# Turning the normed output by DMA, scores in four full banks, and a new order on VectorE, in a retention + MoE block

## The reference, cut to what matters

```python
h = rmsnorm(xn); q, k, v = (h @ ternary(qkv_w).T) split in heads and chunks
def step(S, (qi, ki, vi)):
    scores = einsum('bhtd,bhsd,hts->bhts', qi, ki, mask)      # mask decays and is causal
    o = scale * (einsum('bhts,bhsd->bhtd', scores, vi) + einsum('bhtd,ht,bhde->bhte', qi, lam_t, S))
    kv = einsum('bhtd,ht,bhte->bhde', ki, lam_rev, vi)
    return lam_T * S + kv, o
out = rmsnorm(out, norm_w, 1e-6)
out = rmsnorm(out, proj_norm_w, eps) @ ternary(proj_w).T
```

## Time and profile before

| | |
|---|---|
| median of 3 runs | 1403.2 us (1401.72 to 1403.88) |
| the profiled execution, its own time | 1401.92 us |
| its span | 1400.2 us |
| PE, DVE, ACT, POOL busy over the span | 91%, 50%, 37%, 38% |
| attention steps | from about 76 to 547 us of the span |

### The profile page before, as it was taken

How to read it: one execution, slowest core, us unless ns; L and a number is a source line. 1 busy time by engine, 2 the same in 40 slices (tenths; PEclk the granted TensorE clock), 3 DMA queues, 4 the chain that set the end, 5 groups by cost and what they waited for, 6 DMA issues and landing times. The chain is left out here.

```text
span 1400.2 us, 29499 instructions
## 1 busy us (share of the span) xinstructions
PE 1281.1 (91%) x10418; PEld 879.9 (63%) x10418; DVE 695.2 (50%) x1606; ACT 514.0 (37%) x1034; POOL 527.0 (38%) x467
## 2 busy tenths in 40 slices
PE   1499999999999994999999969999999969999997
PEld 1477777667776673777777734444444447777775
DVE  4477877878878766883333322222222213333323
ACT  3444444444444434432323224544445411111111
POOL 0333344333444332024541035555554542444333
PEclk9699999999999997999999989999999989999999
DMA  5213443334433334524552358888888861443333
GB/s 173 95 60 129 154 145 109 109 131 142 161 109 109 131 125 162 180 93 105 107 138 102 33 136 183 188 194 190 186 191 186 192 190 65 179 164 135 135 136 121
DMA packets 174072, 195.06 MB, mean 139 GB/s; under 512 B 100976, under 2 KB 107248, under 8 KB 174000
## 3 DMA queue, kind: packets, MB, share of 16 engines
q1 hardware_dynamic: 158464, 156.17, 38.0%
q0 software_dynamic: 13328, 37.04, 10.0%
q10 hardware_dynamic: 2208, 0.82, 0.2%
HBM read 117.55 MB, written 56.77 MB: 124 GB/s over the span
## 5 line engine op out<-in xcount | busy, mean ns | idle before, releaser
L1269 PE MATMUL gu<-xT,WG 128*128 128x256 f16 x3072 | 350.3, 275 | 23.5 <-DMA x1s<-x_dram 11.8
L1269 PEld LDWEIGHTS gu<-xT,WG 128*128 128x128 f16 x3072 | 302.7, 99 | 74.8 <-DVE WD L1556 12.4
L1280 PE MATMUL rgu<-WG,raw 128*128 x876 | 215.1, 382 | 14.4 <-issue 10.9
L1695 DVE SCALAR_TENSOR_TENSOR actv<-gu,up_inv,sg 128x512 f32<-128x512 f32 x64 | 48.0, 751 | 252.8 <-ACT sg L1532 252.6
L1532 ACT ACTIVATE sg<-gu,gate_inv 128x512 f32<-128x512 f32 x64 | 43.9, 686 | 319.2 <-PE gu L1269 319.2
L1287 PE MATMUL yp<-WD,ah 128*128 128x512 f16 x512 | 152.3, 379 | 1.0 <-DVE al L1700 1.0
L1280 PEld LDWEIGHTS rgu<-WG,raw 128*128 128x128 f16 x876 | 86.1, 98 | 105.5 <-issue 23.2
L1850 POOL TENSOR_TENSOR xsp<-xg,xsp 128x512 f16<-128x512 f32 x75 | 86.7, 1157 | 105.2 <-ACT xsp L1918 105.2
L655 PE MATMUL ring<-hh,qkvT 128*128 128x256 f16 x512 | 116.4, 276 | 6.0 <-DVE hl L972 6.0
L1250 POOL DMA_INDIRECT xg<-xn_dram,idx x77 | 73.8, 958 | 123.9 <-POOL xsp L1850 66.4
L655 PE MATMUL ring<-hl,qkvT 128*128 128x256 f16 x512 | 116.4, 275 | 0.0
(11 more groups left out here) (237 smaller groups left out, 2163.2 us busy)
## 6 DMA issues: line engine op xcount, KB each, us to landing
y_dram<-raw SPq DMA_DIRECT2D x72, 256.0 KB
xl<-in_L_attn_x SPq DMA_DIRECT2D x16, 512.0 KB, 4.5
xn_dram<-xn SPq DMA_DIRECT2D x16, 512.0 KB, 6.4
wraw<-in_L_ffn_w_gate_up SPq DMA_DIRECT2D x16, 512.0 KB, 6.9
xT_dram<-x SPq DMA_DIRECT2D x16, 512.0 KB, 2.8
xr<-in_L_attn_x SPq DMA_DIRECT2D x16, 512.0 KB, 5.9
x_dram<-x SPq DMA_DIRECT2D x32, 256.0 KB, 2.1
xT<-xT_dram SPq DMA_DIRECT2D x16, 512.0 KB, 6.9
```

What stands on the lines that cost most here:

```text
L1269: ins = pe.matmul(gu[:, h, f * tokens:(f + 1) * tokens], w[:, kk, b, a0:a0 + P], x[:, kk, a], start=(kk == 0 and (a, b) == PASSES[0]), sto ...
L1280: ins = pe.matmul(gu[bank][:], x(kk, a), w[:, 0, kk, b, :], start=(i == 0), stop=(i == len(done) - 1))
L1695: v.scalar_tensor_tensor(out=actv[:, g % 2], in0=gu[g % 2][:, 1].rearrange("p (f t) -> p f t", f=FT), scalar=up_inv[:, 1:2], in1=sg[:], op ...
```

## The change

- `o_turn` and the ring's fills onT0 and onT1 go. ScalarE's `y_high` and VectorE's `y_low` now work on on3 in SBUF, before it is turned, and write the halves ys (128 x 2 x 512, f16); SP turns both halves at once with one DMA transpose per u (`turn_y`) into yT, for which `proj` waits. `store_xT` goes ahead of it in SP's list.
- Scores: all 16 heads of one u in the four full banks, two handovers per u and step instead of four; VectorE's product is 128 x 1024 instead of 128 x 512.
- `masked_kv` leaves VectorE; ScalarE's `take_kv` copies the four diagonal blocks (32 partitions x 4 x 32) in four activations; the rest of kvm is zeroed once by POOL.
- New orders on VectorE and ScalarE; STEP is 18 long, and the second `proj` now waits for `v0`.
- g1 and g2 are made by `tensor_scalar` instead of `tensor_tensor`.

```diff
-    STEP = ["xnT0", "xnT1", "kTr0", "ot0", "kv0", "q0", "q1", "kTr1", "ot1", "rt", "onT0", "k0", "kv1", "k1", "proj0",
-            "onT1", "v0", "v1", None, None, "proj1"]
+    STEP = ["xnT0", "xnT1", "kTr0", "ot0", "kv0", "q0", "q1", "kTr1", "ot1", "rt", "k0", "kv1", "k1", "proj0",
+            "v0", "v1", None, "proj1"]
@@ SP
+            def turn_y(u, q, par):
+                n = 2 * q + par
+                wait_apart(sp, S["yl_ready"], 2 * n + u + 1, S["sp_passed"])
+                sp.dma_start_transpose(yT[:, u], ys[:, u].rearrange("p a c -> p (a c)")).then_inc(yT_in[u], 16)
...
                     load_weights(*after(q, par))
+                    store_xT(*after(q, par))
                 for u in range(B):
-                    if u == 1 and front:
-                        store_xT(*after(q, par))
+                    turn_y(u, q, par)
+                for u in range(B):
@@ TensorE
-                o_turn(0, q, par, st)
...
-                    scores(0, *nxt, (0, 1))
-                o_turn(1, q, par, st)
-                if front:
+                    scores(0, *nxt)
                     project("v0", *nxt, st)
-                    scores(0, *nxt, (2, 3))
                     project("v1", *nxt, st)
                 proj(1, q, par, st)
@@ ScalarE
+            def take_kv(u, q, par, st):
+                n = 2 * q + par
+                bank = filled(act, f"kv{u}", st)
+                act.wait_ge(state_ready[u], n)
+                for j in range(HPT):
+                    own = slice(HD * j, HD * j + HD)
+                    ins = act.activation(kvm[own, u, :, own], bank[own].rearrange("p (g e) -> p g e", g=KT)[:, :, own],
+                                         ACT.Copy)
+                ins.then_inc(S["kvm_ready"], 1)
...
+            def y_high(u, q, par):
+                n = 2 * q + par
+                act.wait_ge(S["on3_ready"], 2 * n + u + 1)
+                act.wait_ge(yT_in[u], 16 * n)
+                act.activation(ys[:, u, 0], on3[:, u], ACT.Copy).then_inc(S["yh_ready"], 1)
...
                 o_root(0, q, par)
+                take_kv(0, q, par, st)
                 if front:
                     take("q0", *nxt, st)
                     take("q1", *nxt, st)
                 on_squares(0, q, par)
+                y_high(0, q, par)
                 take_oT(1, q, par, st)
                 o_square(1, q, par)
-                y_high(0, q, par, st)
+                o_root(1, q, par)
+                if norm:
+                    norm_roots(q + 1, par)
                 if front:
                     take("k0", *nxt, st)
-                o_root(1, q, par)
+                on_squares(1, q, par)
+                y_high(1, q, par)
                 if front:
                     take("k1", *nxt, st)
-                on_squares(1, q, par)
-                if norm:
-                    norm_roots(q + 1, par)
-                y_high(1, q, par, st)
+                take_kv(1, q, par, st)
@@ VectorE, the step as it stands after
+                scaled_k(0, q, par, st)
+                if front:
+                    h_low(*nxt)
+                decayed_scores(1, q, par)
+                o_mean(0, q, par)
+                normed(0, q, par)
+                weight_maxima(q, par, (1, 2, 3))
+                scaled_k(1, q, par, st)
+                second_norm(0, q, par)
+                y_low(0, q, par)
+                if has_norm:
+                    row_stats(0, q + 1, par)
+                    row_stats(1, q + 1, par)
+                if front:
+                    take_logits(*nxt, st)
+                if has_norm:
+                    norm_stats(q + 1, par)
+                o_mean(1, q, par)
+                normed(1, q, par)
+                if has_norm:
+                    norm(q + 1, par)
+                    norm_factors(q + 1, par)
+                second_norm(1, q, par)
+                y_low(1, q, par)
+                weight_maxima(q, par, (0,))
+                residual(0, q, par, st)
+                if front:
+                    decayed_scores(0, *nxt)
+                else:
+                    weight_scales()
+                residual(1, q, par, st)
```

More of the change, by code:

```diff
@@ L497, in attention @@
         xT_out = [sem(c, f"xT_out{i}") for i in range(2)]
+        yT_in = [sem(c, f"yT_in{i}") for i in range(B)]
         wraw_in = [sem(c, f"wraw_in{i}") for i in range(2)]
@@ L657, in project, with scores @@
                 ins.then_inc(done, 1)
-            def scores(u, q, par, sets):
+            def scores(u, q, par):
                 n = 2 * q + par
-                if u == 0 and sets[0] == 0:
+                if u == 0:
                     pe.wait_ge(S["q_ready"], 2 * n + 2)
                     pe.wait_ge(S["k_ready"], 2 * n + 2)
[L664 to L669, removed]
+                for pair in range(2):
+                    pe.wait_ge(sc_free[pair], 2 * n + u)
+                    for g in range(KT):
+                        for j in (2 * pair, 2 * pair + 1):
                             rows = slice(HD * j, HD * j + HD)
-                            ins = pe.matmul(sc[:, j, gg * P:(gg + 1) * P], kT[rows, par, g, u * P:(u + 1) * P],
+                            ins = pe.matmul(sc[:, j, g * P:(g + 1) * P], kT[rows, par, g, u * P:(u + 1) * P],
                                             qT[rows, par, g, u * P:(u + 1) * P], start=True, stop=True)
@@ L690, in outputs @@
                               start=(g == 0), stop=False, skip_group_check=True)
[L691 to L701, removed]
+                for pair in range(2):
+                    pe.wait_ge(sc_free[pair], 2 * n + u + 1)
+                for g in range(KT):
+                    for j in range(HPT):
+                        h = HPT * g + j
+                        ins = pe.matmul(bank[HD * j:HD * j + HD, g * P:(g + 1) * P],
+                                        vS[:, par, u, HD * h:HD * h + HD],
+                                        probs[:, u, j // 2, j % 2, g, :], start=False,
+                                        stop=(g == KT - 1 and j == HPT - 1), skip_group_check=True)
                 ins.then_inc(done, 1)
@@ L720, in outer @@
                 ins.then_inc(done, 1)
[L722 to L728, removed]
             def proj(u, q, par, st):
                 n = 2 * q + par
-                pe.wait_ge(S["yl_ready"], 2 * n + u + 1)
+                pe.wait_ge(yT_in[u], 16 * (n + 1))
                 bank, done = fill(pe, f"proj{u}", st)
                 for g in range(KT):
-                    for y in (yh, yl):
-                        ins = pe.matmul(bank[:], y[:, u, g, :], projT[:, g, :],
-                                        start=(g == 0 and y is yh), stop=(g == KT - 1 and y is yl))
+                    for a in range(2):
+                        ins = pe.matmul(bank[:], yT[:, u, a * KT + g, :], projT[:, g, :],
+                                        start=(g == 0 and a == 0), stop=(g == KT - 1 and a == 1))
                 ins.then_inc(done, 1)
@@ L747, in prologue @@
                     project(name, 0, 0, None)
-                scores(0, 0, 0, (0, 1, 2, 3))
+                scores(0, 0, 0)
                 for name in ("v0", "v1"):
@@ L1018, in weight_scales, with decayed_scores @@
                                        op0=ALU.mult, op1=ALU.mult)
-            def decayed_scores(u, q, par, sets):
+            def decayed_scores(u, q, par):
                 n = 2 * q + par
                 v.wait_ge(S["kscale_ready"], n + 1)
-                for s in sets:
-                    pair = s % 2
-                    v.wait_ge(sc_full[pair], 4 * n + 2 * u + s // 2 + 1)
-                    v.scalar_tensor_tensor(out=probs[:, u, s].rearrange("p (j g) t -> p j (g t)", j=2),
-                                           in0=sc[:, 2 * pair:2 * pair + 2, 0:2 * P],
+                for pair in range(2):
+                    v.wait_ge(sc_full[pair], 2 * n + u + 1)
+                    v.scalar_tensor_tensor(out=probs[:, u, pair].rearrange("p j g t -> p j (g t)"),
+                                           in0=sc[:, 2 * pair:2 * pair + 2],
                                            scalar=r[:, par, u:u + 1],
-                                           in1=mask[:, 4 * s:4 * s + 4].rearrange("p (j g) t -> p j (g t)", j=2),
+                                           in1=mask[:, 8 * pair:8 * pair + 8].rearrange("p (j g) t -> p j (g t)", j=2),
                                            op0=ALU.mult, op1=ALU.mult).then_inc(sc_free[pair], 1)
@@ L1148, in step @@
                 residual(1, q, par, st)
-                if has_norm:
-                    norm_factors(q + 1, par)
             run_steps(v, prologue, step)
@@ L1185, in prologue @@
             def prologue():
+                pool.memset(kvm[:], 0.0)
                 x_low(0, 0)
```

62 lines of the change are left out of this document (15 added, 47 removed).

## The result

The changed kernel takes **1425.53 us** (median, 1419.69 to 1427.19), the kernel before 1402.46 (1400.97 to 1403.88) beside it: a ratio of 1.0157 [1.0125, 1.0189]. So it is 23 us slower. The forecast was 1409 within 1383 to 1430, with slower as the likeliest of the three signs. The profiled execution took 1427.19 us at a span of 1425.4.

A forecast was written before the change was run, and what follows sets the result against it. TensorE's list was taken to set the period by a small margin. Its 3.0 us gain a step returns as one wait, -3 us in all, and clock falls add +10: 1409 us against the profiled 1401.9, range 1383 to 1430.

The forecast's parts named there:

- TensorE, removed: TensorE's list loses o_turn (0.88 us a step) and waits for v1 and scores (2.1): 26.5 us a step, 3.0 less.
- First half and shared wait: First u: normed ends at 10.9 us, over 1 earlier; y_low waits for POOL, starting at 14.4 instead of 14.0.
- Rival 3: POOL goes ahead of y_low, +2 us a step, +30 to +50; or transposes land late, +0.9 a step; chance 0.13.
- The transposes: DMA transposes of the normed output land 3.1 us after issue, before proj wants them, covered by 1.2 and 1.5 us.
- Second half: Second u: POOL holds norm, k1 is copied at 24.3 us, TensorE idles 3.0 before the scores; -0.2 a step.
- Rival 2: VectorE's norm in the second half is not held by POOL: 28.0 us a step, -20 us, 1383; chance 0.15.
- The clock: TensorE's idle time lowers its granted clock, 1.6 us a fall; six falls taken, +10 us, between 0 and +25.
- The likeliest case: TensorE's idle time before the scores with some falls of the clock: 1401 to 1424 us; chance 0.5.
- Rival 1: TensorE's idle time stays but the clock holds: -3 us with an error of 6, 1393 to 1405; chance 0.2.

The follow-up runs named there:

- e6: e3 with the output's turn back on TensorE and the second proj again waiting for the v copy: 1394.29 us, a step of 28.98.
- e3: The changed kernel with ScalarE taking kv1 and k1 early and norm roots last, and VectorE's norm work put behind what the turn needs: 1366.6 us.
- e4: The changed kernel with every DMA transpose issued twice, first into a spare tile: 1421.95 us.
- e9: The changed kernel with the score matmuls of one u issued over all four row groups in turn: 1404.78 us.
- e2: The changed kernel with twelve needless 512-column matmuls filling TensorE's idle time before the scores: 1404.09 us.
- e1: The changed kernel with ScalarE's copy of k1 taken ahead of the squares and y_high(1): 1382.19 us.
- e7: The changed kernel with ScalarE copying kv1 and k1 ahead of the squares and y_high(1), VectorE's order left alone: 1395.52 us.

## Why the prediction was right, and where its sizes were off

**TensorE, removed.** Right: 0.88 of transposes and the wait for v1 are gone, and put back they cost 1.95 a step (e6). I had laid out 26.5 us for TensorE with nothing else to wait for; it is 27.03 (e3), mainly since the scores of one u take 1.65 and not 1.34. That term was twice the 0.67 of sixteen in the earlier trace rows; the pace of sixteen matmuls did not hold for thirty-two.

**First half and shared wait.** Right. The product of 1024 columns takes 1276 ns where I took 1.28. `y_low`(0) and POOL:

```profile
368.82 1.27 POOL L1162 TENSOR_TENSOR state<-state,kvm 128x512 f32<-128x512 f32 x1
...
369.66 0.98 DVE L1074 TENSOR_TENSOR ys<-on,ys 128x512 f16<-128x512 f32 x1
...
370.06 2.80 POOL L1150 TENSOR_TENSOR qlam<-qT,lamq 128x1024 f32<-128x1024 f32 x1
```

`y_low` sits until POOL's L1162 is through (recorded end 370.09) and then runs: 0.98 for the 0.69 that `y_low`(1) takes at 348.00, where POOL is idle. It ends 15.35 behind the second `proj` at 355.29 (laid out: 15.1). POOL's next is 2.80 long instead of the 2.35 of the earlier trace rows: now POOL waits for VectorE. Rival 3, in which POOL goes ahead, is refuted. The Trainium skill (SBUF — State Buffer, "Who interferes with whom") states that a VectorE instruction with two SBUF inputs contends with a GpSimd one that reads SBUF. The 0.98 for 0.69 agrees, for an instruction of 512 columns.

**The transposes.** Right: 3.1 from issue to landing at the median, 4.1 at most (the other half of rival 3, a late landing, is out too), no wait of `proj` in the steady steps, and two of them in a row cost nothing either (e4). Four small copies take 1.09, 0.27 each, where I took 0.26.

```profile
L580 SPq DMA_TRANSPOSE yT<-ys x32: 1232/1242/1422, 91.0 to 558.5; - x32
...
DMA to landing us min/median/max: 3.0/3.1/4.1
```

**Second half.** Right in every link. `norm` was held and ended at 21.8 as laid out (344.39 + 1.88 - 324.41 = 21.9); z2(1) came at 22.8 (22.9), k1 was copied at 24.0 (24.3). Rival 2, `norm` not held, is refuted: 1.88 against the 1.00 of the earlier trace rows. Only the idle time is 2.16 and not 3.0: k1 is 0.2 to 0.3 earlier, and the first `proj` starts at 344.50 - 324.41 = 20.1 instead of 19.6, and its recorded end is 0.16 behind the eight intervals I had counted. That changes nothing in the length of the step, which hangs on k1: the scores start at 24.1, and 24.1 + 1.65 + twice 1.73 = 29.2 (laid out: 29.1). One link was overlooked: the last step with a `front` has no `norm` and so no such wait, fourteen steps have it and not 15.

**The clock.** Here is the failed size. The mechanism (idle time brings half clock, and what follows is on the chain) and its price were right: 1.6 a fall foreseen, 1.66 measured in e9, 1.63 in e4, 1.7 read from the stretches above. The count was not. I took six falls for +10; the trace has one behind every one of the fourteen waits, and two of them twice as long, which the prediction did not have at all. A step of 30.90 less 1.66 is 29.24, 0.2 under the 29.44 of before, and e4's step without a fall is 29.27; the prediction said -0.2. Over the fourteen steps the parts add up: 14 x -0.2 and 16 x 1.66 make +23.8, and from the second `decayed_q` to the last the trace has 435.96 against 412.10, +23.9.

The whole difference of the two profiled executions is 25.2 us of span. Besides the 23.9, the way from the first `decayed_q` to the second is 2.3 shorter, the last step is the same (the prediction took 0 there), and 3.6 lie behind the attention, where the two kernels run the same code: from the last `residual` to the end 856.2 us against 852.6. In the twelve profiled executions of this study that stretch is 851.2 to 856.3 long, so those 3.6 say nothing of the change.

The point forecast, 1409, was 16 us too low. The likeliest case by itself ended at 1424, with all 15 falls; the measured 1425.53 is just above that. It lies within the range because the range was drawn up to 1430 for rival 3, which did not happen. That the number fell inside is in this part luck; the sign and the chain behind it are not.

Rival 1, the idle time without the price, was laid out at 1399, 3 under before. e2 has the full clock but does useless work in the wait, and is 4 over before; less the 0.4 a step by which its matmuls overshoot, that is within the error of 6 that rival 1 allowed.

So the clock alone made the change slower. As work and waits the change is close to a tie, as laid out: TensorE's gain of 3 us comes back as one wait. That this wait is no part of the idea but of two lists shows in e3, which keeps every other part of the change and is 57 us faster.

## What to carry to other kernels

When work leaves the bounding engine, follow what else is behind it on the lists of the engines that took it over: one copy of 0.6 us behind the wrong neighbour cost 41 us here (e1), and moving both engines' lists was worth 57. Price a wait of TensorE twice, once by its length and once by the granted clock in the work behind it, and count the falls pessimistically where the wait recurs in each step: 4 us more of idle time went with 31 us more of run time where the clock fell (the change against e7). When TensorE's own list is what remains, look at the order within a group of small matmuls: turning over all four row groups gave 16 us by the steps (15 of 1.06) and 19 by the medians, for an edit of a few lines.

## What the hardware showed that was not expected

- Matmuls on 32 rows of the array (32x128, f32) depend on how they are interleaved: the 32 of one u (two for each product) took 1.65 us from start to start when the products alternated between two row groups, 1.10 over four, 51 and 34 ns each. In the kernel before sixteen took 0.67, 42 each, eight per pair of groups; the cause of that middle value was not tried.
- The granted clock did not fall behind a wait of 1.88 us before the second `proj` (e7), nor behind 1.07 (e1). It fell behind 2.16 before the scores in every step that had it, and behind 2.46 (e9) only in about two steps of three. In e4 it did not fall behind 0.78 and 1.23 with a `proj` between them, and fell behind 0.39 and 1.61. Length alone does not order these, so something else about the waits must matter; what, was not tried.
- VectorE and POOL, both reading SBUF at once, cost each other in both directions: `norm` took 1.88 beside POOL and 1.00 without it (e3), `y_low` 0.98 and 0.69, and `qlam` 2.80 behind `y_low` and 2.35 before the change.
